# Values in eight products, their rows moved inside SBUF by thirteen transfers a unit

## The reference

```
xl = layer_norm(x over the 192 channels); shift both axes by 3; cut into 7x7 windows (49 tokens)
q, k, v = windows @ qkv_w.T + qkv_b, split into 6 heads of 32 channels
attn = softmax(q k^T / sqrt(32)) over the 49 tokens of a window
out = (attn v) @ proj_w.T + proj_b; windows and shift undone; layer_norm
h = gelu(out @ fc1_w.T + fc1_b) @ fc2_w.T + fc2_b;   result = h + x
```

## Time and profile before

| what | value |
|---|---|
| median of 3 runs | 2929.57 us (2928.83 to 2935.62) |
| profiled execution, own time | 2930.57 us |
| its span | 2928.8 us |
| TensorE, weight loads | 2876.8 us (98%), 2787.5 us (95%) |
| VectorE, ScalarE, GpSimd | 2612.4 us (89%), 2686.3 us (92%), 1287.7 us (44%) |
| transfers | 263.32 MB, 675019 packets; busy 40.9% of 16 engines on the main queue |

### The profile page before, as it was taken

One profiled execution on the slowest core, in us unless ns is written; L12 is line 12 of the kernel. 1 busy time (PEld: TensorE's weight loads), 2 busy tenths in 40 slices (PEclk: granted clock), 3 DMA queues, 4 the chain that ended last, 5 costly groups with the idle time before them and its releaser, 6 DMA issues.

```text
span 2928.8 us, 72487 instructions
## 1 busy us (share of the span) xinstructions
PE 2876.8 (98%) x25004; PEld 2787.5 (95%) x25004; DVE 2612.4 (89%) x7211; ACT 2686.3 (92%) x5500; POOL 1287.7 (44%) x1549
## 2 busy tenths in 40 slices
PE   5999999999999999999999999999999999999998
PEld 4899999999999999999999999999999999999998
DVE  7889999999999999998989898999989999899985
ACT  2899999999999999999999999999999999999996
POOL 3444444444444444444444444444444444444432
PEclk9999999999999999999999999999999999999999
DMA  5344444434443444343444434444443443444431
GB/s 112 81 97 90 89 90 89 99 86 93 95 89 86 94 99 86 85 100 85 92 93 89 97 84 94 95 89 91 92 96 86 94 97 86 94 88 96 87 80 34
DMA packets 675019, 263.32 MB, mean 90 GB/s; under 512 B 505699, under 2 KB 633444, under 8 KB 674660
## 3 DMA queue, kind: packets, MB, share of 16 engines
q1 hardware_dynamic: 670724, 257.00, 40.9%
q10 hardware_dynamic: 3936, 1.68, 0.3%
HBM read 169.23 MB, written 89.27 MB: 88 GB/s over the span
## 4 chain that ended last, share of the span: by engine, by line
PE 81%; SPq 14%; DVE 1%; issue 1%; POOL 1%; DMA 1%; ACT 0%; POOLq 0%; DVEq 0%; ACTq 0%
PE psum L331 8%; PE psum L334 7%; PE psum L332 7%; PE psum L333 7%; PE psum L335 7%; PE psum L623 6%; PE psum L597 5%; PE psum L577 4%; PE psum L578 4%; PE psum L588 4%; PE psum L589 4%; PE psum L579 4%; PE psum L603 4%; SPq L410 3%; SPq L467 3%; PE psum L598 2%
## 5 line engine op out<-in xcount | busy, mean ns | idle before, releaser
L1268 POOL TENSOR_TENSOR pr<-pr,rc 98x294 f32<-98x294 f32 x512 | 384.5, 760 | 371.0 <-DVE rc L1079 371.0
L778 ACT ACTIVATE hh<-psum,b 128x392 fp32r<-128x392 f32 x768 | 451.3, 588 | 32.7 <-PE psum L589 6.4
L781 ACT ACTIVATE hf<-psum,b 128x392 f32<-128x392 f32 x768 | 451.3, 588 | 6.4
L1043 DVE TENSOR_TENSOR hl<-hf,hh 128x392 fp32r<-128x392 f32 x640 | 373.8, 599 | 4.2 <-ACT hf L781 4.1
L1241 POOL TENSOR_TENSOR ve<-mv,eps 104x4 f32<-104x4 f32 (+1 forms) x256 | 81.7, 319 | 660.0 <-DVE mv L1003 660.0
L1066 DVE TENSOR_REDUCE mx<-psum 98x6 f32<-98x294 f32 x512 | 229.1, 447 | 113.8 <-PE psum L598 113.5
L1262 POOL TENSOR_TENSOR hl<-hf,hh 128x392 fp32r<-128x392 f32 x128 | 133.2, 1041 | 358.7 <-ACT hf L781 358.7
L577 PE MATMUL psum<-hh,w2h 128*128 128x392 f32 x768 | 272.4, 355 | 0.0
L735 ACT ACTIVATE pt<-psum 113x294 f32<-113x294 f32 x512 | 205.8, 402 | 68.8 <-PE psum L603 68.6
L597 PE MATMUL psum<-km,qm 128*98 128x98 f32 x2048 | 260.8, 249 | 7.9 <-DVE xn L1008 3.9
L331 PE MATMUL psum<-x_h,w_mh 128*128 128x392 f32 x768 | 265.0, 345 | 0.7 <-DVE pr L1071 0.7
(11 more groups left out here) (135 smaller groups left out, 9929.0 us busy)
## 6 DMA issues: line engine op xcount, KB each, us to landing
bc<-mean_rstd SPq DMA_DIRECT2D x128, 392.0 KB, 3.7
xg<-in_x SPq DMA_DIRECT2D x368, 96.0 KB, 2.4
values_by_token<-vt_m SPq DMA_DIRECT2D x128, 256.0 KB
vbd<-values_by_token SPq DMA_DIRECT2D x256, 96.0 KB
xt<-in_x SPq DMA_DIRECT2D x112, 194.5 KB, 2.8
out<-xt SPq DMA_DIRECT2D x112, 194.5 KB, 3.3
values_by_token<-vt_r SPq DMA_DIRECT2D x128, 128.0 KB
vbd<-values_by_token SPq DMA_DIRECT2D x256, 51.0 KB
```

The source lines that it names most:

```text
L778: nc.scalar.activation(hh[:, m % HB, :], bank("fc1", m)[:, 0:T], ACT.Gelu, bias=b1[:, m:m + 1]).then_inc(s_hh, 1)
L781: nc.scalar.activation(hf[:, m % HB, :], bank("fc1", m)[:, 0:T], ACT.Gelu, bias=b1[:, m:m + 1]).then_inc(s_gelu, 1)
L1268: nc.gpsimd.tensor_tensor(probs(j), probs(j), each, ALU.mult).then_inc(s_prob, 1)
```

## The change

TensorE's `values_rest` has three products in place of five: the weights of high and low part stand beside each other in 128 output columns (wv_m, wv_r), so that PSUM rows 0 to 63 hold the high weights' product and rows 64 to 127 the low weights'. The two halves are still to be added. VectorE transposes all 128 rows. Then SyncE moves the lower half to partitions 0 to 63 (`low_part`) and GpSimd adds it (`last_values`). `values_to_dram` and the tensor in memory are gone. vbd's order is changed (pair of heads outside windows), vt's rows alternate 32 values and 32 zeros, and `spread` copies whole 2 KB rows inside SBUF, per head one transfer of 32 rows and one of 17.

```diff
-VMOVES = 16 * 4
+VMOVES = 16 * 12
+VROW = DH + NW * WP
...
-        vbd = sb("vbd", [128, 2, NW, 3, WP])
+        vbd = sb("vbd", [128, 2, 3, NW, WP])
-        vt_m = sb("vt_m", [128, 2, NW, 2, DH])
-        vt_r = sb("vt_r", [CR, 2, NW, 2, DH])
-        by_token = nc.dram_tensor("values_by_token", [2, C, NW, 2, DH], F32)
+        vt_m = sb("vt_m", [128, 2, 2, VROW])
+        vt_r = sb("vt_r", [128, 2, 2, VROW])
+        vt_l = sb("vt_l", [CR, 2, VROW])
...
+            def low_part(u):
+                sp.wait_ge(s_vt, nth(u, 2, 0))
+                if u > 0:
+                    sp.wait_ge(s_vsum, nth(u - 1, 1, 0))
+                sp.dma_start(vt_l[:, :, DH:], vt_r[CR:128, u % 2, :, DH:]).then_inc(s_vlow, 16)
+            def spread(u):
                 sp.wait_ge(s_vt, nth(u, 2, 1))
                 if u > 1:
                     sp.wait_ge(s_pe["o"], nth(u - 2, 1, 0))
+                for head in range(HEADS):
+                    p, e = head // 2, head % 2
+                    rows, r = (vt_m, DH * head) if head < 4 else (vt_r, DH * (head - 4))
+                    at = DH * (1 - e)
+                    if head == 4:
+                        sp.wait_ge(s_vsum, nth(u, 1, 0))
+                    for b, r0, to, n in ((0, 0, 0, DH), (1, 2 * DH - N, DH, N - DH)):
+                        sp.dma_start(vbd[WP * e + to:WP * e + to + n, u % 2, p], rows[r + r0:r + r0 + n, u % 2, b, at:at + NW * WP]).then_inc(s_vbd[u % 2], 16)
...
                 if 0 <= t - 4 < UNITS:
                     spread(t - 4)
+                if 0 <= t - 3 < UNITS:
+                    low_part(t - 3)
                 if 0 <= t - 1 < UNITS:
                     if t - 1 > 0:
                         stats_out(t - 1)
-                if 0 <= t - 3 < UNITS:
-                    values_to_dram(t - 3)
...
-                claim(u, [("vt", 0)], (s_lo["x1"], 2, 1))
-                five(bank("vt", 0)[0:CR, 0:T], wq, CM, CR, [p[:, :] for p in x1]).then_inc(s_pe["vt"], 1)
+                claim(u, [("vt", 0)], (s_lo["x1"], 2, 0))
+                ps = bank("vt", 0)[:, 0:T]
+                nc.tensor.matmul(ps, wv_m[:, :], x1[0][:, :], start=True, stop=False)
+                nc.tensor.matmul(ps, wv_m[:, :], x1[1][:, :], start=False, stop=False)
+                pe.wait_ge(s_lo["x1"], nth(u, 2, 1))
+                nc.tensor.matmul(ps, wv_r[:, :], x1[2][:, :], start=False, stop=True).then_inc(s_pe["vt"], 1)
...
+                if n == 0:
+                    for pair, raw_, of in ((wv_m, sm_, w[0]), (wv_r, sr_, w[2])):
+                        nc.vector.tensor_copy(pair[:, 0:CR], of[:, CM:C].bitcast(F32))
+                        nc.vector.tensor_tensor(pair[:, CR:128], raw_[:, CM:C], of[:, CM:C].bitcast(F32), ALU.subtract)
...
-                    dve.wait_ge(s_vd, 16 * 2 * (u - 1))
+                    dve.wait_ge(s_vbd[u % 2], nth(u // 2 - 1, VMOVES, VMOVES - 1))
...
+            def last_values(u):
+                pool.wait_ge(s_vlow, 16 * (u + 1))
+                nc.gpsimd.tensor_tensor(of_blocks(vt_r[0:CR, u % 2]), of_blocks(vt_r[0:CR, u % 2]), of_blocks(vt_l), ALU.add).then_inc(s_vsum, 1)
...
                     if u[1] > 0:
                         times_rstd_rest(u[1])
+                if u[2] is not None:
+                    last_values(u[2])
                 if u[4] is not None:
                     rstd(1, u[4])
...
+            for t in (vt_m, vt_r):
+                nc.gpsimd.memset(t[:], 0.0).then_inc(s_zero_qk, 1)
```

More of the change, by code:

```diff
@@ L136, in swin_block_program @@
         w1 = [sb(f"w1_{p}", [128, NF], F32R) for p in ("mh", "ml", "rh", "rl")]
+        wv_m = sb("wv_m", [128, 128], F32R)
+        wv_r = sb("wv_r", [128, 128], F32R)
         w2h = sb("w2h", [128, MT, C], F32R)
@@ L242, in swin_block_program @@
         s_vt = sem("values_by_token")
-        s_vd = sem("values_in_dram")
+        s_vlow = sem("low_part_of_last_values_moved")
+        s_vsum = sem("last_values_summed")
         s_vbd = [sem(f"vbd_ready_{i}") for i in range(2)]
@@ L372, in norm_vector, with of_blocks @@
                               vec[CM:C].rearrange("(p a) -> p a", a=1)).then_inc(loaded, 16)
+        def of_blocks(rows):
+            return rows[:, :, DH:].rearrange("p b (w c) -> p w b c", w=NW)[:, :, :, 0:DH]
         def o_rest(t, r0, wi):
@@ L447, in _ @@
             sp.dma_start(b2[0:CR, 1:2], fc2_b[CM:C].rearrange("(p a) -> p a", a=1)).then_inc(s_rest, 16)
-            def values_to_dram(u):
+            def low_part(u):
[4 more added lines that the diff above has]
+            def spread(u):
                 sp.wait_ge(s_vt, nth(u, 2, 1))
                 if u > 1:
[L454 to L461, removed]
-                    sp.wait_ge(s_pe["o"], nth(u - 2, 1, 0))
[L464 to L468, removed]
+                    sp.wait_ge(s_pe["o"], nth(u - 2, 1, 0))
+                for head in range(HEADS):
[6 more added lines that the diff above has]
+                        sp.dma_start(vbd[WP * e + to:WP * e + to + n, u % 2, p], rows[r + r0:r + r0 + n, u % 2, b, at:at + NW * WP]).then_inc(s_vbd[u % 2], 16)
             for t in range(UNITS + 7):
@@ L531, in _ @@
             pe.wait_ge(s_zero, 1)
-            pe.wait_ge(s_zero_qk, 5)
+            pe.wait_ge(s_zero_qk, 7)
             pe.wait_ge(s_split, 1)
@@ L622, in weighted @@
                     block, side = (wi, p) if p < 2 else (2, wi)
-                    last = nc.tensor.matmul(ps, vbd[0:KP, u % 2, 2 * j + wi, p, :], pt[:, j, block, N * side:N * side + N],
+                    last = nc.tensor.matmul(ps, vbd[0:KP, u % 2, p, 2 * j + wi, :], pt[:, j, block, N * side:N * side + N],
                                             start=True, stop=True)
@@ L766, in hi_part @@
                     act.wait_ge(s_zero, 1)
-                    act.wait_ge(s_zero_qk, 5)
+                    act.wait_ge(s_zero_qk, 7)
                     act.wait_ge(s_bias, 2)
@@ L1082, in v_out @@
                 if u > 1:
-                    dve.wait_ge(s_vd, 16 * 2 * (u - 1))
+                    dve.wait_ge(s_vbd[u % 2], nth(u // 2 - 1, VMOVES, VMOVES - 1))
                 dve.wait_ge(s_pe["vt"], nth(u, 2, c))
-                blocks = bass.AP(psum, BANK_OF["vt", c] * 512, [[8 * 512, (CR, CM)[c]], [N, NW], [N - DH, 2], [1, DH]])
-                nc.vector.transpose((vt_r, vt_m)[c][:, u % 2], blocks).then_inc(s_vt, 1)
+                blocks = bass.AP(psum, BANK_OF["vt", c] * 512, [[8 * 512, 128], [N, NW], [N - DH, 2], [1, DH]])
+                nc.vector.transpose(of_blocks((vt_r, vt_m)[c][:, u % 2]), blocks).then_inc(s_vt, 1)
             def step(t, k, it):
```

## The result

The changed kernel takes 3477.42 us (3473.42 to 3481.87, 4 runs) against 2931.15 for the kernel before (4 runs); the ratio is 1.186 with a 95% interval of [1.184, 1.188]. Forecast were 3327 and a range of 2990 to 3560.

A forecast was written before the change was run, and what follows sets the result against it. TensorE was taken to bound the kernel at 22.27 us a step. The new loop's terms summed to 25.6 us, over 120 steps +400 us, so 3327 us was forecast, range 2990 to 3560.

The forecast's parts named there:

- a loop of SyncE, one transfer, GpSimd's sum and residual: Residual, store, loads, means, spreads, low_part, sum, next residual: claimed to close over one step at 25.6 us, against 22.27 today.
- 17-row transfers make a line on one engine: SyncE's spreads: 17-row transfers aren't divided, so low_part waits behind them on one transfer engine; 122 pieces, 9.8 us.
- The two things that I was least sure of: Transfers inside SBUF: that 2 KB rows go at 80 ns each, and that low_part can't pass them.
- The length: The loop's terms summed to one step: 25.6 us, bounds 24.0 to 28.5.
- store to the means' issue: SyncE's stores, loads and groups up to the issue of the means: 7.3 us, bounds 6.9 to 7.9.
- Means' issue to the sum: From SyncE's issue of the means to GpSimd's sum: 3.2 for the means, 9.8 for 122 pieces, 0.5 to the semaphore.
- Sum and tail: GpSimd's sum with its start, 1.4 us, and then from L1241 to the end of residual, 3.3 us.
- The issue of 0.4 us: SyncE's cost to issue one spread, taken as 0.4 us, 4.8 us for twelve; held not to matter if data is slower.
- Rival 3: SyncE's issues at 0.63 us close the loop though data is shared out: 22.6 us a step, 2990 us; chance 0.07.
- TensorE's 0.36 us: values_rest on TensorE: three products for five at 0.178 us each save 0.36 us a step.
- the 45 us of gain: TensorE's saving over 128 steps: 45 us less if TensorE stays the bound.
- Rival 4: The loop, and TensorE's clock dropping to the 1.2 GHz level on top: some 27.5 us a step, 3555 us; chance 0.08.

The follow-up runs named there:

- e1: Changed kernel with low_part issued ahead of the twelve spreads of its step, not behind them: 2916.34 us, ratio 0.9931 to the kernel before.
- e4: Changed kernel with last_values at the end of GpSimd's step, behind residual and the last scaled_probs: 2925.45 us, ratio 0.9959 to the kernel before.
- e3: Changed kernel with five products as before, no low_part and no sum, the twelve spreads kept: 2923.06 us, ratio 0.9952 to the kernel before.
- e2: Changed kernel with 16 rows in place of 17 in the second transfer of every head: 3209.97 us, ratio 1.093 to the kernel before.
- e5: Changed kernel with six more transfers a unit, each of 16 rows, into a tile that nobody reads: 3613.22 us.
- e6: Changed kernel with six more transfers a unit, each of 17 rows, into a tile that nobody reads: 4523.86 us.

## Why the prediction was right, step by step

- **That a loop of SyncE, one transfer, GpSimd's sum and residual closes over one step** was right: e1 and e4 each cut it at another place and all of the loss is gone, e3 leaves out the sum with the same effect.
- **That 17-row transfers make a line on one engine, and low_part stands in it** was right: e2, e5 and e6. The two things that I was least sure of measured 84 ns a piece between e6 and the changed kernel and 82 ns in the line's own row (80 forecast), and a landing that follows the pieces.
- **The length** was 25.6, measured 26.74, just above the 25 to 26 named as a sign of being right. The term mis-sized most is store to the means' issue: 7.3, measured 8.25, beyond even its bounds of 6.9 to 7.9. I counted the issues at their clean length. A turn of 13 clean issues takes 7.12 us, as the one shown does; two turns of each image have 15 or 16 issues, which adds 0.3 on the mean, and in four turns of five single issues are longer, which adds 0.8 (in the turn after the one shown an L434 takes 2.02). What makes single issues long was not tried. Means' issue to the sum was 13.5, measured 14.26: 122 x 4 ns = 0.5, and 0.3 in the start. Sum and tail were 0.5 too long, so part of the errors cancel.
- **The issue of 0.4 us** was wrong: 0.60 at the median and 0.64 with what lies between two. That the sum came out in spite of it was luck in this one term, since the line was slower still. Rival 3 (no line, issues at 0.63) had its price right in kind and too small: 22.6 us a step forecast, 24.7 measured in e2. I had written that nothing of the issues matters "if data is slower than issue"; e2 shows that the issues alone are enough to be slower than before. That the line alone would be too is an estimate: 26.74 us is the line's length from means to sum plus the other terms, and short issues would not shorten it. No run has the line without the issues.
- **TensorE's 0.36 us**, the term behind the 45 us of gain, was 0.30 in its own row and 0.16 in the step (e1). I had seen ScalarE's slack of 0.2 to 0.5 us a step, but as a sum over the step; the slack that decided was 0.34 us at one bank.
- **Rival 4**, the clock: TensorE's mean granted clock is 0.945, from 0.997. It waits and runs partly at the 1.2 GHz level, but isn't in the loop, and the loop's terms add up to the whole step without it. In e6 it is 0.843, and the step is still the loop's.

## What to carry to other kernels

A new wait costs what stands behind it, and what that in turn releases: follow it around until it comes back to its own transfer, add the loop's terms, and compare the sum with the step of the engine that bounds the kernel. Before dropping such a change, move the transfer ahead of the bulk or the waiting operation behind the one that others need; here two lines turned +18.6% into -0.7%. Slack is to be read at the instruction that waits, not as idle time over a step.

## What the runs showed of the hardware that I had not expected

- Issuing a transfer from SBUF to SBUF took SyncE's queue, at the median from 800 to 2600 us, 0.61 us at 17 rows, 0.51 at 32 rows and 0.68 at 64 rows of two pieces in the changed kernel, and 0.59 at 16 and at 32 rows and 0.68 at 64 in e2, where no line stood on one engine. Between SBUF and memory 64 to 128 rows took 0.34 to 0.58. Few rows didn't make an issue cheap.
- The 256 KB of low_part took 3.2 us from issue to landing where no line stood before them (the median in e1, e2 and e5), not the 2.0 of a 3.8 KB load.
- The product after the weighted sums starts its successor only after 0.28 us with 128 weight columns (e1), and after 0.23 with 64 (the kernel before), both against 0.18 for the others. Why was not tried.
